# Order of work where stages meet in a four-layer attention and mixture kernel: norm transposes into the banks of keys and units, dense products around the last probabilities, the last norm tile one step later

## The chip, the cores and the metric

The kernel runs on one core of a Trainium2 chip. The core has five engines that each take their instructions in order and meet only at semaphores: TensorE (PE, matrix products; PEld is its weight load), VectorE (DVE), ScalarE (ACT), GpSimd (POOL) and SyncE (SP, which issues the DMAs). The metric is the device time of one execution in microseconds.

## The reference

`x` is 16 x 64 tokens of width 512, `ctx` as many. Four layers follow each other, each an attention and a mixture, each with a residual add and a layer norm ahead of it:

```python
x = x + _L0_xattn_ref(_layernorm(x), ctx, Wq, Wk, Wv, Wo)    # 32 heads, 4 key heads, keys = ctx and x
x = x + _L0_ffn_ref(_layernorm(x), base_W, gate_W, A, B)      # xf @ base_W.T + low-rank experts, top 2 of 28
x = x + _L1_xattn_ref(_layernorm(x), ctx, mask, ...)          # 32 heads, 8 key heads, rms-normed q and k
x = x + _L1_ffn_ref(_layernorm(x), W_base, gate_W, A, B)      # the same with top 2 of 8
x = x + _L2_xattn_ref(_layernorm(x), ctx, ctx)
x = x + _L2_ffn_ref(_layernorm(x), router_w, A, B)
x = x + _L3_xattn_ref(_layernorm(x), ctx, ...)
x = x + _L3_ffn_ref(_layernorm(x), weight, bias, centroids, assignments)

def _L0_ffn_ref(x, base_W, gate_W, lora_A, lora_B):
    base = xf @ base_W.T
    top_vals, top_idx = jax.lax.top_k(xf @ gate_W.T, TOP_K)
    top_probs = jax.nn.softmax(top_vals / TEMP, axis=-1)
    gate_full = zeros.at[arange, top_idx].add(top_probs)
    h = einsum('nd,erd->ner', xf, lora_A) * (gate_full * SCALING)[:, :, None]
    return base + einsum('ner,eor->no', h, lora_B)
```

## The kernel before

The 1024 tokens are eight tiles of 128 rows (`NT` = 8); `x` stays in SBUF. Every product is made in single precision out of three passes over a high and a low half of each operand (`PASSES`): ScalarE copies the high half (`..._hi`), VectorE or GpSimd subtracts it for the low half (`..._lo`, `low`).

**Attention.** `attention(a, next_ln)` runs 64 steps (`STEPS`; 8 head groups by 8 tiles) and one more, then a tail. Step t works on four tiles at once: projections of step t, `scores` of t-1, `p_transpose` and `attend` of t-2, `out_proj` of t-3. In the first layer the queries are made in units (`q_unit`) into the banks psQ and psT, half of the heads for two tiles each. psTP is two banks, psT and psP.

**Norms.** A tile's norm is `ln_stats` (VectorE), `ln_rstd` (GpSimd), `ln_norm` into `xn` (VectorE), `ln_transpose` (TensorE, four transposes into the bank that `ln_bank` names), `ln_hi` (ScalarE) and `ln_lo` (VectorE). The next layer's norm begins inside the attention: tiles 0 to 4 at steps 60 to 64 (`LN_SLOT`), tiles 5 and 6 in the tail, tile 7 in the loop after it.

**Mixture.** `ffn_step(f, next_ln, t)` runs for t = 0 to 10: `gate_product(f, t)` into psQ, `gates` (some ten small instructions of VectorE with one `gate_exp` of ScalarE between) that give `hid`, `hidden_transpose`, `hidden_hi`, `hidden_lo`, then `experts` onto the same bank as `dense_product(f, t)`. `ring3` names that bank, one of three. `experts_add` adds it to `x`.

**What sets the order.** Nothing but the order of the code in each engine's block; a wait on a semaphore holds all that stands behind it on that engine. At the end of an attention TensorE has `scores`, `p_transpose`, `out_proj` and `attend` of the last steps, and as work that depends on none of them the first gate and dense products and the norm transposes.

**The start.** SyncE loads `x` tiles 0 and 1, four slices of the first query weights, the context, the first key weights and then the other six tiles. GpSimd makes the low halves of two slices of the query weights (`low_wq`), of half the context (`low_ctx`) and of the key weights (`low_wkv`), VectorE the others. `idle_products(n)` are n products whose result nobody reads.

Names with a number in the rows below: L775 `q_unit`, L790 `q_proj`, L812 `kv_proj`, L822 `q_transpose`, L840 `p_transpose`, L850 and L856 `attend`, L869 `out_proj`, L706 `ln_transpose`, L720 `gate_product`, L733 `dense_product`, L955 `hidden_transpose`, L971 `experts`, L1721 every low half on VectorE, L488 every low half on GpSimd.

## Time and profile before

| what | us |
|---|---|
| median of 3 runs (1569.87 to 1570.59) | 1570.47 |
| the profiled execution, its own time | 1570.53 |
| its span, first to last instruction | 1568.7 |
| TensorE busy | 1501.3 |
| VectorE busy | 1008.9 |
| ScalarE busy | 821.1 |
| GpSimd busy | 379.4 |

The profiled execution spends 1.83 us outside its span. The first attention runs to about 641 us, its mixture to 686, the second attention to 1301, its mixture to 1346. A row of a timeline gives the start, the length, engine, line, operation, the tiles out<-in, shape and count, and in brackets how long the engine stood idle before it and who released it. Matrix products overlap, so the distance of two starts tells what one costs in a row of work.

### The profile page before, as it was taken

To read this page: it belongs to the slowest core of one execution; us is meant where nothing else is said; L and a number is where in the kernel's file an instruction comes from. 1 tells how busy PE (TensorE), PEld (TensorE's weight loads), DVE (VectorE), ACT (ScalarE), POOL (GpSimd) and SP (SyncE) were. 2 spreads that over 40 slices of the span, in tenths; PEclk is the share of its full clock that TensorE was granted. 3 is DMA by queue.
4 is the path that set the end of the run, shared out by engine and by line. 5 is a ranking of instruction groups with operands and counts; after the bars stand their busy time and mean duration, and the time that the engine had idled before them with its cause. 6 is when DMAs were issued, how large, how long until landed. Compare 5 with 4: busy or idle time off the path is not lost.

```text
span 1568.7 us, 27791 instructions
## 1 busy us (share of the span) xinstructions
PE 1501.3 (96%) x9658; PEld 1323.4 (84%) x9658; DVE 1008.9 (64%) x2475; ACT 821.1 (52%) x2862; POOL 379.4 (24%) x388
## 2 busy tenths in 40 slices
PE   7999999999999998999999999999999998879896
PEld 7899999999999997788888888888888887667785
DVE  6666556655665568766665666656666677688775
ACT  4556445644555455346565556555565652554542
POOL 4102010201111011133232332323232321543420
PEclk9999999999999999999999999999999998799998
DMA  4100100100011001010101010101100001111001
GB/s 182 62 28 28 42 28 28 56 14 28 28 55 36 33 13 41 28 41 28 41 28 41 28 50 19 68 8 62 41 28 32 5 8 55 44 55 35 24 11 57
DMA packets 14624, 60.21 MB, mean 38 GB/s; under 512 B 2085, under 2 KB 3493, under 8 KB 9497
## 3 DMA queue, kind: packets, MB, share of 16 engines
q1 hardware_dynamic: 14488, 58.46, 10.5%
q8 instruction: 79, 1.29, 0.4%
q14 instruction: 57, 0.46, 0.1%
HBM read 56.36 MB, written 2.10 MB: 37 GB/s over the span
## 4 chain that ended last, share of the span: by engine, by line
PE 59%; issue 27%; DVE 7%; POOL 3%; ACT 2%; DMA 1%; POOLq 0%; DVEq 0%; SPq 0%; ACTq 0%
PE psY L869 15%; PE psQ L790 11%; PE psKV L812 8%; PE psSO L759 3%; PE psSO L856 2%; PE psTP L822 2%; PE psQ L775 2%; PE psTP L775 2%; PE psSO L760 2%; POOL wo L488 1%; PE psTP L840 1%; PE psKV L733 1%; PE psQ L1137 1%; PE psQ L720 1%; PE psTP L706 1%
## 5 line engine op out<-in xcount | busy, mean ns | idle before, releaser
L869 PE MATMUL psY<-wo,oT 128*128 128x512 f32 x1536 | 384.9, 399 | 1.8 <-DVE oT L1721 1.2
L869 PEld LDWEIGHTS psY<-wo,oT 128*128 128x128 f32 x1536 | 278.6, 188 | 65.8 <-POOL wo L488 2.2
L488 POOL TENSOR_TENSOR wo<-stage_o,wo 128x512 fp32r<-128x512 f32 (+2 forms) x71 | 91.1, 1309 | 309.0 <-ACT wo L1275 309.0
L1275 ACT ACTIVATE pT<-psTP 128x512 fp32r<-128x512 f32 (+1 forms) x128 | 62.8, 491 | 169.4 <-PE psTP L840 169.4
L593 POOL TENSOR_TENSOR rms<-ms_eps,minus_half 128x5 f32<-128x5 f32 x64 | 74.7, 1168 | 280.2 <-DVE ms_eps L1884 277.2
L1356 ACT ACTIVATE prob<-wide,neg_mx 128x128 f32<-128x128 f32 x256 | 99.8, 391 | 75.0 <-DVE neg_mx L1871 74.8
L1353 ACT ACTIVATE prob<-s_sb,neg_mx 128x64 f32<-128x64 f32 x256 | 86.0, 337 | 98.3 <-DVE neg_mx L1871 98.3
L1721 DVE TENSOR_TENSOR pT<-psTP,pT 128x512 fp32r<-128x512 f32 (+1 forms) x128 | 71.3, 557 | 77.4 <-ACT pT L1275 76.4
L1721 DVE TENSOR_TENSOR v<-psKV,v 128x128 fp32r<-128x128 f32 x64 | 18.7, 292 | 140.4 <-ACT v L1275 140.4
L812 PEld LDWEIGHTS psKV<-wkv,arena 128*128 128x128 f32 x768 | 99.8, 190 | 9.0 <-DVE kT L1908 4.6
L812 PE MATMUL psKV<-wkv,arena 128*128 128x256 f32 x768 | 103.4, 284 | 1.2 <-DVE kT L1908 1.2
L790 PE MATMUL psQ<-wq,hT 128*128 128x512 f32 x384 | 104.0, 408 | 0.0
L775 PE MATMUL psQ<-hT,wq 128*128 128x256 f32 x768 | 99.6, 285 | 4.2 <-DVE hT L1721 2.9
L790 PE MATMUL psQ<-hT 128*128 128x512 f32 x372 | 100.1, 407 | 0.0
L775 PEld LDWEIGHTS psQ<-hT,wq 128*128 128x128 f32 x768 | 94.9, 192 | 5.9 <-DVE hT L1721 3.1
L812 PE MATMUL psKV<-wkv,hT 128*128 128x256 f32 x768 | 99.8, 286 | 0.0
L775 PE MATMUL psTP<-hT,wq 128*128 128x256 f32 x768 | 99.1, 286 | 0.0
L1275 ACT ACTIVATE oT<-psSO 128x512 fp32r<-128x512 f32 (+1 forms) x132 | 76.4, 579 | 38.8 <-PE psY L869 32.1
L775 PEld LDWEIGHTS psTP<-hT,wq 128*128 128x128 f32 x768 | 96.0, 195 | 0.0
L812 PEld LDWEIGHTS psKV<-wkv,hT 128*128 128x128 f32 x768 | 94.1, 192 | 0.3
L1326 ACT ACTIVATE pT<-psQ 128x128 fp32r<-128x128 f32 x252 | 66.3, 280 | 53.4 <-PE psQ L790 53.4
L1721 DVE TENSOR_TENSOR oT<-psSO,oT 128x512 fp32r<-128x512 f32 (+1 forms) x132 | 88.7, 672 | 7.5 <-ACT oT L1275 7.2
(303 smaller groups left out, 3389.5 us busy)
## 6 DMA issues: line engine op xcount, KB each, us to landing
stage_o<-in_wo SPq DMA_DIRECT2D x16, 1024.0 KB, 4.8
stage_q<-in_wq SPq DMA_DIRECT2D x15, 1024.0 KB, 5.3
stage_kv<-in_wkv SPq DMA_DIRECT2D x12, 512.0 KB, 3.6
stage_q<-in_ctx SPq DMA_DIRECT2D x16, 256.0 KB, 2.8
stage_o<-in_ctxT SPq DMA_DIRECT2D x2, 1024.0 KB, 5.8
stage_q<-in_base SPq DMA_DIRECT2D x2, 1024.0 KB, 4.9
...
```

Source lines behind the costliest of these rows:

```text
L488: g.tensor_tensor(dst[LO], stage, dst[HI].bitcast(f32), ALU.subtract).then_inc(ld[done or what + "_lo"], 1)
L593: g.tensor_tensor(rms[:, t.res(2)], ms_eps[:, t.res(2)], minus_half[:, 0:5], ALU.pow).then_inc(s["rms"], 1)
L759: mm(bank[:, at:at + 2 * keys], q_of(HI), k_of(slice(0, 2)), start=True, stop=False)
L775: m = mm(out, wq[:, wl, c, head], lat_pair(xl, c, k.res(NT) // 2), start=c == 0 and i == 0, stop=c == KT - 1 and i == 2)
L790: m = mm(by_eight(q_bank(st)[:]), lat(xl, k, n), wq_slice(st.div(NT) + a.wq0, wl, k), start=k == 0 and i == 0, stop=k == KT - 1 and i == 2)
L812: m = mm(psKV[:, b * 256:(b + 1) * 256], lhsT, wkv_k(wl, k, 256), start=k == 0 and i == 0, stop=k == KT - 1 and i == 2)
L869: m = mm(psY[:], oT[:, ol, h, :], wo[:, wl, h, :], start=h == 0 and i == 0, stop=h == HQ - 1 and i == 2)
L1275: copy = lambda o, i: nc.scalar.activation(o, i, ACT.Copy)
L1326: i = nc.scalar.activation(junk_q[h], q_bank(st)[:, h * HD:(h + 1) * HD], ACT.Square, accum_out=ssq[:, n, h:h + 1])
L1353: e = nc.scalar.activation(prob[:, at], s_sb[:, at], ACT.Exp, bias=neg_mx[:, j:j + 1], scale=1.0, accum_out=sums[:, j:j + 1])
L1356: e = nc.scalar.activation(prob[:, at], wide[:, at], ACT.Exp, bias=neg_mx[:, j:j + 1], scale=a.scale, accum_out=sums[:, j:j + 1])
L1721: return V.tensor_tensor(dst_lo, src, dst_hi.bitcast(f32), ALU.subtract)
```

## The change

It rewrites the order on all five engines at three places, with a few buffers moved so that the order is possible. What is computed stays the same, but for nine more idle products at the start.

- **Start.** `x` tiles 2 and 3 come in a DMA of their own ahead of the context, which then waits for the third weight slice. GpSimd takes a third slice of `low_wq` from VectorE and computes tiles 2 and 3's `ln_rstd` ahead of `low_ctx`; VectorE normalises tiles 2 and 3 ahead of its own `low_ctx`. 14 idle products in place of 5.
- **End of the first attention and its mixture.** The norm transposes of tiles 0 to 2 go to psKV, behind `out_proj` in place of ahead of it. `gate_product(0)` moves one step ahead; `dense_product(0)` stands behind the p_transpose of step 64 and `dense_product(1)` behind the last one; `hidden_transpose(0)` and `gate_product(1)` are in the tail, `dense_product(2)` one step later behind the transpose of tile 7. The halves of the experts' matrix are kept in `kT1` and `v1` in place of `wo`, and are made earlier (`high_b`, `low_b`). The base weights' halves (`next_wq`, `low_wq(8)`) are made behind the norm's in step 62.
- **Second attention.** The last `experts` of the first mixture stands inside the first `q_proj`; the transpose of norm tile 7 stands behind the second `q_proj`. At its end `gate_product(0)` moves ahead of `out_proj(61)`, `dense_product(0)` ahead of `attend(62)`, `dense_product(1)` ahead of the last `p_transpose`, and the mixture's head is as above; its experts' matrix is in the context part of `hT`.

The diff, cut to the lines that set the order:

```diff
-        if ln in (1, 3, 7):
-            return psT if n == NT - 1 and ln != 7 else psP
+        if ln == 1:
+            return psKV if n < 3 else psT
+        if ln in (3, 7):
+            return psT if n >= 4 and ln != 7 else psP
+        if ln == 2 and n == NT - 1:
+            return psP
...
-        return (psS, psKV, psY)[n % 3]
+        return (psKV, psS, psY)[n % 3]
...
+        sp.dma_start(x[:, 2:4], io["x"][:, 2:4]).then_inc(ld["x23"], 16)
+        sp.wait_ge(ld["slot2"], 16)
...
-        sp.dma_start(x[:, 2:NT], io["x"][:, 2:NT]).then_inc(ld["x_rest"], 16)
+        sp.dma_start(x[:, 4:NT], io["x"][:, 4:NT]).then_inc(ld["x_rest"], 16)
...
+        low("wq", halves(wq, 2), stage_q[:, 2], 3, "wq_lo_v")
+        ln_rstd(0, 2)
+        ln_rstd(0, 3)
...
-        for n in range(2, NT):
+        for n in range(4, NT):
...
-            if n == 3:
+            if n == 2:
                 low_wq(8)
+            if n == 5:
+                low_b(FF[0], 32)
...
+            if t.t == STEPS - 2:
+                low_b(FF[1], 66)
...
+            if f.index == 0 and t == 0:
+                pe.wait_ge(LNS[1]["lo"], ln_at(1, 3))
...
-                    pe.wait_ge(FS["x_add"], NT)
+                    pe.wait_ge(FS["x_add"], NT - 1)
...
-                        if not t.exists:
-                            gate_product(f, 0)
+                    if t1.exists and t.exists and not units:
+                        gate_product(f, 0)
...
+                    if not t.exists:
+                        dense_product(f, 0)
...
-                if a.norm_slot(t) == "between":
+                if a.rms and a.norm_slot(t) == "between":
...
+                if a.rms and not t.exists:
+                    gate_product(f, 0)
...
+                if not a.rms and a.norm_slot(t) == "between":
+                    ln_transpose(next_ln, t.t - LN_SLOT, lambda: ln_bank_free(next_ln, t.t - LN_SLOT, t2))
...
+                    dense_product(f, 0)
...
-                    ln_transpose(2, NT - 1, lambda: pe.wait_ge(LNS[2]["lo"], ln_at(2, NT - 1)))
+                    q_proj(t.back(-1), 0, 4)
+                    ln_transpose(2, NT - 1, lambda: None)
                 if t.exists and a.rms:
-                    if t.t < 2:
+                    if t.t == 1:
...
+            if not a.rms:
+                p_transpose(last)
+            pe.wait_ge(s["max"], last.c + 1)
+            dense_product(f, 1)
             if a.rms:
-                gate_product(f, 0)
-            pe.wait_ge(s["max"], last.c + 1)
-            dense_product(f, 0)
-            p_transpose(last)
+                p_transpose(last)
...
+            hidden_transpose(f, 0)
             ln_transpose(next_ln, 5, lambda: ln_bank_free(next_ln, 5, last))
-            dense_product(f, 1)
+            gate_product(f, 1)
...
-                if t == 1:
-                    pe.wait_ge(A["x_add"], (f.index + 1) * STEPS)
-                    dense_product(f, 2)
-                    ln_transpose(f.ln, NT - 1, lambda: None)
-                if t > 2:
+                    if t == 2:
+                        ln_transpose(f.ln, NT - 1, lambda: pe.wait_ge(LNS[f.ln]["lo"], ln_at(f.ln, NT - 1)))
+                        pe.wait_ge(A["x_add"], (f.index + 1) * STEPS)
                     dense_product(f, t)
-            if 0 <= u < NT:
+            if 0 <= u < NT - (f.index == 0):
...
-        idle_products(5)
+        idle_products(14)
...
-                if t.exists and not a.rms and not early and t.res(8) == 6:
+                if t.exists and not a.rms and not early and t.res(8) == 6 and t.t < LN_SLOT:
...
-                if a.norm_slot(t) == "between":
+                if a.rms and a.norm_slot(t) == "between":
                     ln_hi(next_ln, t.t - LN_SLOT)
+                if a.rms and t.t == STEPS:
+                    gate_exp(FF[1], 0)
+                if a.rms and t.t == STEPS:
+                    oT_hi(t2)
...
-                if t2.exists and a.rms:
+                if not a.rms and t.t == STEPS - 1:
+                    gate_exp(FF[0], 0)
+                if not a.rms and a.norm_slot(t) == "between":
+                    ln_hi(next_ln, t.t - LN_SLOT)
+                if t2.exists and t.exists and a.rms:
...
+                if not a.rms and t.t == STEPS - 2:
+                    next_wq(t)
...
+                if a.rms and t.t == STEPS - 3:
+                    high_b(FF[1], 17)
+                if not a.rms and t.t == STEPS:
+                    high_b(FF[0], 8)
...
-            gate_exp(FF[a.index], 0)
             oT_hi(last)
-            for n in range(5, NT - 1):
-                ln_hi(next_ln, n)
+            hidden_hi(FF[a.index], 0)
+            ln_hi(next_ln, 5)
+            gate_exp(FF[a.index], 1)
+            ln_hi(next_ln, 6)
...
-                for n in first:
+                for n in first if t.t > 0 else ():
...
+                    pT_lo(t2)
...
-                if t2.exists:
+                if t2.exists and not scores_first:
                     pT_lo(t2)
+                if a.rms and t.t == STEPS:
+                    gates(FF[1], 0)
...
-                if a.norm_slot(t) == "between":
+                if a.rms and a.norm_slot(t) == "between":
...
-                if t.exists and not a.rms and t.res(8) == 6:
+                if t.exists and not a.rms and t.res(8) == 6 and t.t < LN_SLOT:
                     low_wq(t.div(8) + 1)
+                ahead = a.rms and not t.exists
+                if ahead:
+                    x_add(t3)
+                    oT_lo(t2)
...
-                if t3.exists:
+                if not a.rms and t.t == STEPS - 1:
+                    gates(FF[0], 0)
+                if t3.exists and not ahead:
                     x_add(t3)
-                if t2.exists and a.rms:
+                if not a.rms and a.norm_slot(t) == "between":
+                    ln_lo(next_ln, t.t - LN_SLOT)
+                if t2.exists and a.rms and not ahead:
...
+                if not a.rms and t.t == STEPS - 2:
+                    low_wq(8)
...
-            gates(FF[a.index], 0)
...
+            hidden_lo(FF[a.index], 0)
...
+            gates(FF[a.index], 1)
...
-        def hidden_lo(f, n):
-            dve.wait_ge(FS["hidT_hi"], f.done + n + 1)
-            sub_hi(hidT[0:f.rows, LO, 0:f.parts], hid_bank(f, n)[0:f.rows].rearrange("p (j t) -> p j t", t=P),
-                   hidT[0:f.rows, HI, 0:f.parts]).then_inc(FS["hidT_lo"], 1)
...
-        low_wq(0, 2)
...
-        low_ctx(0)
...
+        ln_norm(0, 2)
+        ln_norm(0, 3)
+        low_ctx(0)
```

The changed file has other line numbers: L1770 there is L1721 here, L729 is L706, L743 L720, L758 L733, L870 L840, L899 L869, L997 L955 and L1013 L971.

**Start, VectorE.** Before, from the first normalised tiles to the queries of the first unit (x_res is `x`, stage_q the loaded query weights, stage_o the loaded context):

```order
L1721 TENSOR_TENSOR wq<-stage_q,wq 128x512
L1721 TENSOR_TENSOR hT<-psY,hT 128x4x128
L1721 TENSOR_TENSOR wq<-stage_q,wq 128x512
L1721 TENSOR_TENSOR hT<-psTP,hT 128x4x128
L1721 TENSOR_TENSOR hT<-stage_o,hT 128x4x2x64 x2
L1743 BN_STATS bn<-x_res 128x6
L1744 BN_AGGR mv<-bn 128x2
L1745 TENSOR_SCALAR var_eps<-mv 128x1
L1743 BN_STATS bn<-x_res 128x6
L1744 BN_AGGR mv<-bn 128x2
L1745 TENSOR_SCALAR var_eps<-mv 128x1
L1762 TENSOR_SCALAR xn<-x_res,mv,rstd 128x512 x2
```

and now:

```order
L1770 TENSOR_TENSOR hT<-psY,hT 128x4x128
L1770 TENSOR_TENSOR wq<-stage_q,wq 128x512
L1770 TENSOR_TENSOR hT<-psTP,hT 128x4x128
L1792 BN_STATS bn<-x_res 128x6
L1793 BN_AGGR mv<-bn 128x2
L1794 TENSOR_SCALAR var_eps<-mv 128x1
L1792 BN_STATS bn<-x_res 128x6
L1793 BN_AGGR mv<-bn 128x2
L1794 TENSOR_SCALAR var_eps<-mv 128x1
L1811 TENSOR_SCALAR xn<-x_res,mv,rstd 128x512 x2
L1770 TENSOR_TENSOR hT<-stage_o,hT 128x4x2x64 x2
```

One weight slice has left VectorE's list, and the statistics and the normalising of tiles 2 and 3 stand ahead of the two context slices.

**End of the first attention, TensorE.** Before, from the gate product of tile 0 (psQ<-wkv,hT) through the dense products 0 and 1 (psSO and psKV<-wq,hT):

```order
L720 MATMUL psQ<-wkv,hT 128x252 x12
L840 MATMUL psTP<-ident,prob 128x128 x4
L869 MATMUL psY<-wo,oT 128x512 x12
L850 MATMUL psSO<-pT,arena 128x256 x6
L706 MATMUL psTP<-ident,xn 128x128 x4
L733 MATMUL psSO<-wq,hT 128x512 x12
L840 MATMUL psTP<-ident,prob 128x128 x4
L869 MATMUL psY<-wo,oT 128x512 x12
L850 MATMUL psSO<-pT,arena 128x256 x6
L706 MATMUL psTP<-ident,xn 128x128 x4
L733 MATMUL psKV<-wq,hT 128x512 x12
L869 MATMUL psY<-wo,oT 128x512 x12
```

and now, from the same p_transpose as the second row above; the gate product of tile 0 stands one step further ahead:

```order
L870 MATMUL psTP<-ident,prob 128x128 x4
L758 MATMUL psKV<-wq,hT 128x512 x12
L899 MATMUL psY<-wo,oT 128x512 x12
L880 MATMUL psSO<-pT,arena 128x256 x6
L729 MATMUL psTP<-ident,xn 128x128 x4
L870 MATMUL psTP<-ident,prob 128x128 x4
L758 MATMUL psSO<-wq,hT 128x512 x12
L899 MATMUL psY<-wo,oT 128x512 x12
L880 MATMUL psSO<-pT,arena 128x256 x6
L997 MATMUL psTP<-ident,s_sb 112x128 x2
L729 MATMUL psTP<-ident,xn 128x128 x4
L743 MATMUL psQ<-wkv,hT 128x252 x12
```

Dense product 0 has moved between a p_transpose and the `out_proj` behind it, dense product 1 stands behind the last p_transpose, and a hidden transpose (s_sb) and the gate product of tile 1 stand ahead of the last `out_proj`.

**Head of the second mixture, TensorE.** Before, from the norm transpose of tile 6 to the dense product of tile 3 (psSO<-hT):

```order
L706 MATMUL psTP<-ident,xn 128x128 x4
L720 MATMUL psQ<-wkv,hT 128x72 x12
L955 MATMUL psTP<-ident,s_sb 64x128
L733 MATMUL psY<-hT 128x512 x12
L706 MATMUL psTP<-ident,xn 128x128 x4
L971 MATMUL psSO<-wo,oT 128x512 x3
L955 MATMUL psTP<-ident,s_sb 64x128
L720 MATMUL psQ<-wkv,hT 128x72 x12
L971 MATMUL psKV<-wo,oT 128x512 x3
L955 MATMUL psTP<-ident,s_sb 64x128
L720 MATMUL psQ<-wkv,hT 128x72 x12
L733 MATMUL psSO<-hT 128x512 x12
```

and now, from the same place:

```order
L729 MATMUL psTP<-ident,xn 128x128 x4
L1013 MATMUL psKV<-hT,qT 128x512 x3
L997 MATMUL psTP<-ident,s_sb 64x128
L743 MATMUL psQ<-wkv,hT 128x72 x12
L729 MATMUL psTP<-ident,xn 128x128 x4
L758 MATMUL psY<-hT 128x512 x12
L1013 MATMUL psSO<-hT,oT 128x512 x3
L997 MATMUL psTP<-ident,s_sb 64x128
L743 MATMUL psQ<-wkv,hT 128x72 x12
L758 MATMUL psKV<-hT 128x512 x12
```

Gate product 1 is in the tail, experts 0 (psKV<-hT,qT) comes first, and the transpose of tile 7 and dense product 2 (psY<-hT) now stand between gate product 2 and experts 1, where there was no dense product.

## Rows read from the trace of the kernel before

**Rows 1.** The page, part 1: busy time of each engine.

```profile
PE 1501.3 (96%) x9658; PEld 1323.4 (84%) x9658; DVE 1008.9 (64%) x2475; ACT 821.1 (52%) x2862; POOL 379.4 (24%) x388
```

**Rows 2.** Windows: stretch, length, busy of PE, PEld, DVE, ACT, POOL, PEclk, DMA.

```profile
52.00:583.70 531.70, 529.88 (x3809) 496.51 (x3808) 313.25 (x584) 276.14 (x832) 62.67 (x48) 1.00 0.09 31
583.70:694.86 111.16, 101.91 (x614) 88.25 (x613) 86.96 (x233) 51.01 (x128) 26.24 (x29) 1.00 0.12 42
1279.80:1322.31 42.51, 36.82 (x186) 29.26 (x185) 30.00 (x105) 9.25 (x31) 5.43 (x10) 0.88 0.15 50
1310.80:1322.31 11.51, 8.91 (x28) 6.92 (x29) 6.59 (x34) 0.98 (x5) 1.63 (x4) 0.56 0.15 49
1349.00:1366.00 17.00, 13.14 (x62) 12.33 (x61) 7.29 (x19) 7.53 (x17) 8.84 (x12) 0.51 0.11 32
```

**Rows 3.** Timeline of TensorE at the start.

```profile
11.99 3.14 PE L775 MATMUL psQ<-hT,wq 128*128 128x256 f32 x24 [2.87 <-DVE hT L1721]
18.96 1.12 PE L706 MATMUL psTP<-ident,xn 128*128 128x128 f32 x4 [3.82 <-DVE xn L1762]
...
20.58 4.71 PE L775 MATMUL psTP<-hT,wq 128*128 128x256 f32 x24
25.13 3.04 PE L812 MATMUL psKV<-wkv,hT 128*128 128x256 f32 x24
```

**Rows 4.** Timeline of VectorE at the start.

```profile
8.73 1.41 DVE L1721 TENSOR_TENSOR wq<-stage_q,wq 128x512 fp32r<-128x512 f32 x1 [1.50 <-ACT wq L1275]
...
10.66 0.68 DVE L1721 TENSOR_TENSOR wq<-stage_q,wq 128x512 fp32r<-128x512 f32 x1
...
16.26 0.69 DVE L1743 BATCH_NORM_STATS2 bn<-x_res 128x6 f32<-128x512 f32 x1 [0.80 <-DMA x_res<-in_x]
...
18.35 1.23 DVE L1762 TENSOR_SCALAR xn<-x_res,mv,rstd 128x512 f32<-128x512 f32 x2
```

**Rows 5.** Timeline of GpSimd at the start.

```profile
6.83 2.75 POOL L488 TENSOR_TENSOR wq<-stage_q,wq 128x512 fp32r<-128x512 f32 x2 [0.18 <-ACT wq L1275]
...
14.87 2.93 POOL L488 TENSOR_TENSOR wkv<-stage_kv,wkv 128x512 fp32r<-128x512 f32 x2
```

**Rows 6.** Who TensorE waited for in 583 to 611: total, times, longest.

```profile
PE psTP L706 <- DVE pT L1721: 2.3, 3, 1.0
```

**Rows 7.** Timeline of TensorE at the end of the first attention.

```profile
621.13 1.61 PE L720 MATMUL psQ<-wkv,hT 128*128 128x252 f32 x12
...
626.50 0.60 PE L706 MATMUL psTP<-ident,xn 128*128 128x128 f32 x4
626.85 3.00 PE L733 MATMUL psSO<-wq,hT 128*128 128x512 f32 x12
629.69 0.60 PE L840 MATMUL psTP<-ident,prob 128*128 128x128 f32 x4
```

**Rows 8.** Timeline of TensorE, three places of the first join.

```profile
619.00 0.98 PE L850 MATMUL psSO<-pT,arena 128*128 128x256 f32 x6 [1.97 <-DVE pT L1721]
...
652.31 0.43 PE L955 MATMUL psTP<-ident,s_sb 128*112 128x128 f32 x2 [1.34 <-DVE s_sb L1778]
...
694.86 0.60 PE L822 MATMUL psTP<-ident,q_sb 128*128 128x128 f32 x4
```

**Rows 9.** Timeline of VectorE, a norm and a query tile of this join.

```profile
616.78 1.57 DVE L1762 TENSOR_SCALAR xn<-x_res,mv,rstd 128x512 f32<-128x512 f32 x1
...
693.53 0.68 DVE L1892 TENSOR_TENSOR q_sb<-psQ,rms 128x512 f32<-128x512 f32 x1
```

**Rows 10.** Timeline of TensorE in the second mixture.

```profile
1313.40 0.42 PE L955 MATMUL psTP<-ident,s_sb 128*64 128x128 f32 x1 [2.61 <-DVE s_sb L1778]
1313.50 2.75 PE L720 MATMUL psQ<-wkv,hT 128*128 128x72 f32 x12
1316.06 5.42 PE L733 MATMUL psSO<-hT 128*128 128x512 f32 x12
...
1322.31 0.30 PE L955 MATMUL psTP<-ident,s_sb 128*64 128x128 f32 x1
```

89 lines of the change are left out of this document (50 added, 39 removed).

## The prediction, made before the change was run

> **What bounds the kernel now.** I read the page first: TensorE is busy 1501.3 us [rows 1] of a span of 1568.7, the others far less. So only two things can move the time: TensorE's idle and the clock it runs at, since the change takes no product away. Next the windows [rows 2]: from 52 to 583.7 us TensorE is busy 529.88 of 531.70 at full clock, and nothing is to be had. The stretch where the first attention hands over to its mixture and to the second attention (583.70 to 694.86) has 111.16 - 101.91 = 9.25 us of idle, the end of the second attention with the head of its mixture (1279.80 to 1322.31) 42.51 - 36.82 = 5.69 us and a granted clock of 0.88. Then the timelines, for who is late in each.
>
> **The start.** The idle of 3.82 us ahead of the transposes of norm tiles 2 and 3 [rows 3] ends with VectorE's xn at 18.35, whose statistics begin at 16.26, when the DMA has landed [rows 4]; the clock has fallen meanwhile: the unit behind it takes 4.71 us, the one ahead 3.14 [rows 3]. I walk the new order. GpSimd does two weight slices from 6.83 in 2.75 us, so 1.37 each; a third ends at 6.83 + 4.1 = 10.95 [rows 5]. VectorE's one remaining slice is ready at about 9.85 and reads stage_q and wq as GpSimd does. The trace has such a slice at 1.41 us beside GpSimd and 0.68 alone [rows 4]; 8.73 + 1.41 is 0.56 past GpSimd's end at 9.58, so I take it as held until GpSimd ends: 10.95 + 0.68 = 11.6. The low half of norm tile 1 ends 0.6 later, and the first unit starts at 12.25 in place of 11.99: the slice taken off VectorE gains nothing here. The unit ends at 15.3. Statistics of tiles 2 and 3 take 18.35 - 16.26 = 2.1 us [rows 4], from 12.2 to 14.3 (512 KB of x ahead of the context have landed by then: the 1536 KB behind it landed at 16.26); rstd and xn add 0.6 each, so the transposes run from 15.4 to 16.1, and the second unit follows at once, without the clock's fall, to 19.0. The first key product needs GpSimd's context and key slices. They end now about 14.9 + 2 x 2.93 = 20.8 (a pair of slices 2.93 [rows 5], the context's like the keys'; they wait for rstd of tile 3). So it starts at 20.85 in place of 25.13 [rows 3]: **4.3 us** gained. New idle there is 20.85 - 19.0 = 1.8 us; nine more idle products run in an idle that exists. Ends: if the slices do not collide, the first unit starts at 11.2 and all is 1.1 earlier (5.4); if the clock falls in the 1.8 us, about as before, 4.71 - 3.14 = 1.6 is given back (2.7). The Trainium skill (SBUF — State Buffer, section "Who interferes with whom") says that a VectorE instruction with two SBUF inputs fully blocks against a GpSimd one that reads SBUF. By that rule the slice ends at 11.6 as above; if the row's 1.41 were a mere slowing it would end at 9.85 + 1.41 = 11.3 and the start would gain 0.3 more.
>
> **End of the first attention.** (a) Norm transposes of tiles 0 to 2 waited for the low half of pT, which frees psP: 2.3 us in three waits [rows 6]. In psKV behind `out_proj` they wait for neither it nor xn (ready before out_proj's 2.84 us are over), so all of that goes and TensorE is 2.0 us early at the scores of step 62; it loses 0.3 there to the low half of the last unit. (b) VectorE is next late. Of the wait of 1.97 us ahead of attend [rows 8] one part was xn at 1.57 us in place of 0.55, held by GpSimd's weight slices [rows 9]. That collision goes, but VectorE's own two slices, 0.68 each [rows 4], now run at that time, and the first waits about 0.4 for GpSimd's; so pT's low half comes at 617.4, TensorE has arrived at 615.5, and it waits 1.9 us again. `out_proj(60)` ahead of it waits 0.85. (c) Behind that stand gate product 0 (622.57 - 621.13 = 1.44) and dense product 0 (629.69 - 626.85 = 2.84) [rows 7] as cover: dense 0 hides the ten small instructions of the gates, which now stand ahead of x_add and the low half of oT (2.1 us). `attend(62)` waits 0.7 and the last p_transpose 0.85. (d) In the tail hidden transpose 0, gate product 1 and experts 0 are covered; the transpose of tile 7 waits about 1.3 for the last statistics, rstd and xn; the wait of 1.34 for hid at 652.31 [rows 8] goes. By this walk TensorE is at that hidden transpose at 649.0: 3.3 us ahead. `high_b`, `low_b` (2.7 us of GpSimd) run while VectorE and TensorE need nothing of either; the rstd behind them on GpSimd is asked for 3 us later. If that cover is gone, it costs up to 2.7 us.
>
> **Head of the second attention.** The last experts inside q_proj takes away its wait for the low half (0.5). The transpose of tile 7 behind the second q_proj takes away its wait for xn (0.45). But VectorE has that tile's low half ahead of q_sb of step 0 in its list: the chain transpose, high half (0.6), low half (0.7), q_sb (0.68 [rows 9]) now starts only when the q_proj is over, and q_transpose waits 2.0 us, where it followed at once at 694.86 [rows 8]. It starts at about 692.45, so this join gives **2.4 us**. Count: 9.25 us of idle become 0.25 + 0.85 + 1.9 + 0.7 + 0.85 + 1.3 + 2.0 = 7.85, four stops fewer at 0.15 each: 2.0, near the walk's 2.4. Bounds: 4.4 if the low half of tile 7 is out of q_sb's way, -1 if VectorE is a microsecond later at three of its stops than I have it.
>
> **Second attention's end.** Gate product 0 (1.4) ahead of `out_proj(61)` covers the wait for oT; dense 0 covers attend's pT; x_add and oT's low half are ahead of the last normalise, and dense 1 covers that. By the walk I find none of these waits left up to hid of tile 1 (0.4). The tile-7 transpose waits for the last statistics: 1.45. Then dense 2 (2.84) stands between gate product 2 and hid of tile 2, where 2.61 us were waited [rows 10]: the gates of tile 2 end at 1309.2 and TensorE arrives at 1309.2. Idle 5.69 to 1.85 is 3.85, and 0.3 for three stops fewer. With the wait goes what followed it: from 1310.80 the clock was at 0.56 [rows 2], the dense product took 5.42 against 3.00 at full [rows 7, 10], the gate product 2.75, about half of it lost: 2.4 + 1.3 = 3.7 us. Together **7.8 us**: TensorE at hidden transpose 3 at 1314.5 in place of 1322.31 [rows 10]. Bounds: 4.1 if the clock falls all the same in the waits that are left, 8.5 if the 1.45 are shorter. Behind it nothing is changed; the half clock of 1349 to 1366 [rows 2] stays in the sum as it was.
>
> **Sum.** 4.3 + 2.4 + 7.8 = 14.5 us. The profiled execution took 1570.53, within 0.1 of the median 1570.47: **1556.0 us**.
>
> **Rivals.** (1) The clock takes part back. New idle of 1.8 us at the start, and 1.3, 1.45 and 0.4 at the heads, may bring half clock for a while as 2.61 us did: 1.6 to 3.7 us, so 1557.6 to 1559.7. For it: idles of this size are left; against: the 1.97 us at 617 [rows 8] and all else of the 9.25 us of the first join ran at full clock [rows 2]. The Trainium skill (TensorE: Matmul & The Clock Gate, section "A second HAM failure mode: psum-queue depth-cycling") tells of a clock that swings when the engine idles shortly but often between groups of products; by that rule this rival would hold at all three places. (2) VectorE bounds both ends: it is busy 86.96 of the 111.16 us and 30.00 of the 42.51 [rows 2], in chains, so cover in TensorE's order only moves the stop. Then the first join gives nothing and the second 1.5 less: 1560. For it: rows 8 and 9; against: a fifth to a third of its time in both stretches is still idle. (3) The half clock of 1349 to 1366 does not come back, since it hangs on when the idle falls: 13.14 us busy at 0.51 would save some 4 net of waits: 1552. (4) **Slower than before.** Each us of product at half clock costs one more. If the stops of the first join (0.85, 1.9, 0.7, 0.85 within 15 us) let the clock fall at 612 and it stays down into the mixture, whose dense and gate products run to 686, each 1 us of full-speed work there costs 1 more; more than 14.5 + 3.1 = 17.6 us of them, so half clock until about 650, makes 1573.6 or more. Against it: the fall at 1310.8 mended itself after some 10 us of unbroken work. (5) It does not do what it says, the covers sit where nothing waits: within 0.2% of before.
>
> **How the numbers follow.** Forecast 0.57; (1) 0.17; (2) 0.13; (3) 0.07; (4) 0.03; (5) 0.03. The forecast's own spread from the bounds (the start 2.7 to 5.4, join 1 -1 to 4.4, join 2 4.1 to 8.5) is about 2.5 us each way. The range reaches from (3), 1551.5, to (2) with a microsecond over, 1561.0. A measurement can tell about 0.2%, 3.1 us, from no change: faster 0.93, same 0.04, slower 0.03.
>
> **What would show it.** Right: the first L812 product near 20.9 with a second unit of 3.1 us; no wait of the norm transposes at steps 60 to 62; attend of step 61 still waiting near 2 us for pT; q_transpose of the second attention waiting 2 us for q_sb; hidden transpose 3 of the second mixture at full clock, 14 us earlier than before. Wrong: a granted clock below 0.9 in the windows around 18 to 25 or 1290 to 1310, or stops for oT or hid in the tails that I have at none.

## The result

| | before | after |
|---|---|---|
| median of 12 runs | 1571.06 | 1563.16 |
| lowest to highest | 1569.75 to 1574.84 | 1557.71 to 1568.28 |
| the profiled execution, its span | 1568.7 | 1560.7 |
| mean granted clock in it | 0.985 | 0.984 |

The ratio is 0.995, 95% interval 0.994 to 0.996: 7.9 us faster, where 14.5 was forecast, and 2.2 us outside the range. Half clock below means the lower of the two levels at which TensorE's clock is granted, 1.2 in place of 2.4 GHz, a PEclk of 0.5 in the windows. Two things stand out before any row. The kernel after spreads over 10.6 us, more than the 7.9 us that it gained. And its mean granted clock is no better than that of the kernel before, though 5.3 of the 14.5 us were to come from the clock (3.7 in the second mixture, 1.6 at the start).

The page of after, parts 1 and 2 (TensorE is as busy as in [rows 1], but for some idle products and for products that ran at half clock):

```profile
PE 1505.0 (96%) x9676; PEld 1326.3 (85%) x9676; DVE 1006.9 (65%) x2474; ACT 819.2 (52%) x2862; POOL 381.2 (24%) x389
...
PEclk9999999999999999999999999999999999799998
```

How far after is ahead of before at the same product of the program, from both timelines of TensorE:

| the product | before | after | ahead by | forecast |
|---|---|---|---|---|
| first key product | 25.13 | 21.06 | 4.07 | 4.3 |
| hidden transpose 2, first mixture | 652.31 | 644.87 | 7.44 | 7.6 |
| q_transpose of step 0, second attention | 694.86 | 687.83 | 7.03 | 6.7 |
| q_transpose of step 3 | 717.85 | 713.24 | 4.61 | 6.7 |
| q_transpose of step 63 | 1279.25 | 1274.75 | 4.50 | 6.7 |
| hidden transpose 3, second mixture | 1322.31 | 1311.44 | 10.87 | 14.5 |
| first attend of the cross-attention | 1465.93 | 1454.92 | 11.01 | 14.5 |
| end of the span | 1568.7 | 1560.7 | 8.0 | 14.5 |

Up to 687.83 us the walk holds to a third of a microsecond. From there 6.8 us are lost, 6.5 against the forecast since after was 0.3 ahead of it. They go in three steps: 2.5 behind the second attention's head, nearly all within 25 us, 1.4 in the second join (6.37 gained, not 7.8), 2.9 behind 1419 us, where the two kernels have the same instructions.

The windows of after, for the same stretches (columns as in [rows 2]; the last three are stretches cut out at half clock):

```profile
579.70:687.83 108.13, 101.47 (x617) 88.22 (x615) 84.61 (x233) 49.95 (x130) 26.49 (x29) 1.00 0.12 44
687.83:713.24 25.41, 22.44 (x128) 19.30 (x129) 13.79 (x40) 15.29 (x71) 8.53 (x7) 0.87 0.12 40
1275.30:1311.44 36.14, 34.25 (x186) 27.26 (x185) 28.95 (x105) 8.42 (x30) 4.18 (x9) 0.95 0.03 10
1419.00:1560.70 141.70, 124.77 (x649) 99.46 (x648) 95.38 (x251) 58.88 (x152) 40.51 (x56) 0.94 0.10 34
...
689.20:692.70 3.50, 3.26 (x16) 3.26 (x16) 0.88 (x2) 1.61 (x12) 0.00 (x0) 0.52 0.02 5
1300.20:1303.70 3.50, 3.06 (x10) 2.62 (x11) 3.29 (x16) 0.84 (x3) 0.81 (x2) 0.52 0.00 0
1453.80:1460.70 6.90, 5.78 (x14) 4.53 (x15) 2.79 (x7) 1.59 (x4) 0.81 (x2) 0.51 0.14 40
```

and of before, for the second and the fourth of these:

```profile
694.86:720.00 25.14, 21.87 (x142) 18.42 (x141) 15.65 (x43) 16.49 (x74) 9.83 (x8) 1.00 0.13 43
1430.00:1568.70 138.70, 120.69 (x649) 96.08 (x649) 95.34 (x251) 58.89 (x152) 40.49 (x56) 0.97 0.10 35
```

The head of the second attention had a clock of 1.00 in the kernel before and has 0.87 now; the second join 0.88 before [rows 2], now 0.95; what lies behind 1419 us (1430 before) had 0.97 and has 0.94. The second join parts waits from clock: TensorE's idle there went from 5.69 to 1.89 us (36.14 - 34.25), where 1.85 was forecast, but its busy time fell only from 36.82 to 34.25, 2.57 us, where 4.0 was forecast (3.7 of clock and 0.3 for stops fewer). In each of the three losses there is half clock. TensorE's timeline of after there:

```profile
685.23 0.60 PE L729 MATMUL psTP<-ident,xn 128*128 128x128 f32 x4
687.83 0.66 PE L850 MATMUL psTP<-ident,q_sb 128*128 128x128 f32 x4 [2.01 <-DVE q_sb L1946]
...
689.44 2.93 PE L840 MATMUL psKV<-wkv,arena 128*128 128x256 f32 x12 [0.84 <-DVE kT L1962]
...
702.31 0.67 PE L850 MATMUL psTP<-ident,q_sb 128*128 128x128 f32 x4 [1.71 <-DVE q_sb L1946]
702.80 0.39 PE L857 MATMUL psKV<-ident,k_sb 128*128 128x128 f32 x1
702.85 2.91 PE L818 MATMUL psQ<-hT 128*128 128x512 f32 x6
...
1300.64 1.11 PE L729 MATMUL psTP<-ident,xn 128*128 128x128 f32 x4 [1.33 <-DVE xn L1811]
1301.41 4.00 PE L758 MATMUL psY<-hT 128*128 128x512 f32 x12
...
1454.92 1.65 PE L1188 MATMUL psY<-kT,pT 128*128 128x512 f32 x3 [2.67 <-DVE pT L1770]
```

and of before, at the second, fourth and last of these:

```profile
696.41 1.69 PE L812 MATMUL psKV<-wkv,arena 128*128 128x256 f32 x12 [0.84 <-DVE kT L1908]
...
707.93 0.66 PE L822 MATMUL psTP<-ident,q_sb 128*128 128x128 f32 x4 [1.71 <-DVE q_sb L1892]
708.42 0.27 PE L829 MATMUL psKV<-ident,k_sb 128*128 128x128 f32 x1
708.45 1.63 PE L790 MATMUL psQ<-hT 128*128 128x512 f32 x6
...
1465.93 0.96 PE L1152 MATMUL psY<-kT,pT 128*128 128x512 f32 x3 [2.67 <-DVE pT L1721]
```

Read them in pairs. The same twelve key products take 1.69 and 2.93 us behind the same stop of 0.84; after has its new stop of 2.01 us 1.6 us ahead of them, which before has not. The same q_transpose, behind the same stop of 1.71, is followed by full clock before and by half clock after. The same attend behind the same stop of 2.67 took 0.96 and takes 1.65. The stops were read rightly; for the last two, what the clock does behind them is not the same each time.

### The profile page after: what moved, and what is told of

It is laid out like the page before. It is cut to its first block, busy times and chain, and to the rows that moved or that the text cites. A ratio compares the mean times of both kernels' runs of the same rounds, so it can differ in the third digit from the quotient of the medians.

```text
span 1560.7 us, 27827 instructions
## 1 busy us (share of the span) xinstructions
PE 1505.0 (96%) x9676; PEld 1326.3 (85%) x9676; DVE 1006.9 (65%) x2474; ACT 819.2 (52%) x2862; POOL 381.2 (24%) x389
## 4 chain that ended last, share of the span: by engine, by line
PE 60%; issue 26%; DVE 8%; POOL 3%; ACT 2%; DMA 0%; SPq 0%; POOLq 0%; DVEq 0%; ACTq 0%
PE psY L899 14%; PE psQ L818 11%; PE psKV L840 8%; PE psSO L787 3%; PE psSO L886 2%; PE psTP L850 2%; PE psSO L788 2%; PE psQ L803 1%; POOL wo L506 1%; PE psTP L870 1%; PE psTP L803 1%; PE psSO L758 1%; PE psQ L1173 1%; PE psKV L1217 1%; DVE hT L1770 1%
## 5 line engine op out<-in xcount | busy, mean ns | idle before, releaser
L899 PE MATMUL psY<-wo,oT 128*128 128x512 f32 x1536 | 384.7, 399 | 1.4 <-DVE oT L1770 0.8
L899 PEld LDWEIGHTS psY<-wo,oT 128*128 128x128 f32 x1536 | 278.3, 188 | 65.7 <-POOL wo L506 2.3
L506 POOL TENSOR_TENSOR wo<-stage_o,wo 128x512 fp32r<-128x512 f32 x68 | 87.3, 1313 | 309.2 <-ACT wo L1311 309.2
L1770 DVE TENSOR_TENSOR pT<-psTP,pT 128x512 fp32r<-128x512 f32 (+1 forms) x128 | 71.2, 556 | 75.9 <-ACT pT L1311 75.1
L1770 DVE TENSOR_TENSOR v<-psKV,v 128x128 fp32r<-128x128 f32 x64 | 18.6, 291 | 142.3 <-ACT v L1311 142.3
L840 PEld LDWEIGHTS psKV<-wkv,arena 128*128 128x128 f32 x768 | 101.0, 192 | 8.3 <-DVE kT L1962 3.7
L840 PE MATMUL psKV<-wkv,arena 128*128 128x256 f32 x768 | 104.5, 286 | 0.8 <-DVE kT L1962 0.8
L840 PE MATMUL psKV<-wkv,hT 128*128 128x256 f32 x768 | 99.9, 286 | 1.0 <-POOL wkv L506 1.0
L840 PEld LDWEIGHTS psKV<-wkv,hT 128*128 128x128 f32 x768 | 94.0, 192 | 1.5 <-POOL wkv L506 1.2
L506 POOL TENSOR_TENSOR wq<-stage_q,wq 128x512 fp32r<-128x512 f32 x35 | 44.9, 1294 | 204.5 <-ACT wq L1311 165.8
```

The costliest lines, as they stand in the source:

```text
L506: g.tensor_tensor(dst[LO], stage, dst[HI].bitcast(f32), ALU.subtract).then_inc(ld[done or what + "_lo"], 1)
L840: m = mm(psKV[:, b * 256:(b + 1) * 256], lhsT, wkv_k(wl, k, 256), start=k == 0 and i == 0, stop=k == KT - 1 and i == 2)
L899: m = mm(psY[:], oT[:, ol, h, :], wo[:, wl, h, :], start=h == 0 and i == 0, stop=h == HQ - 1 and i == 2)
L1770: return V.tensor_tensor(dst_lo, src, dst_hi.bitcast(f32), ALU.subtract)
```

## Experiments

Two theories. **Clock**: the walk over waits was right, and half clock behind TensorE's stops took back what it had given. **Waits**: something in the order that the walk missed (VectorE's chains, a stop that moved) costs the 6.5 us. Medians, spreads and mean granted clocks of the single runs:

| kernel | median | lowest to highest (n) | clocks | ratio to before, 95% |
|---|---|---|---|---|
| after | 1563.16 | 1557.71 to 1568.28 (12) | 0.980 to 0.989 | 0.995 [0.994, 0.996] |
| e1_start | 1569.52 | 1565.87 to 1571.93 (12) | 0.983 to 0.990 | 0.998 [0.997, 0.999] |
| e2_head_order | 1557.42 | 1553.64 to 1562.34 (6) | 0.983 to 0.993 | 0.992 [0.990, 0.993] |
| e3_head_fill | 1562.18 | 1557.37 to 1565.23 (6) | 0.983 to 0.993 | 0.994 [0.992, 0.996] |
| e5_all_fill | 1562.18 | 1561.43 to 1563.27 (6) | 0.994 to 0.997 | 0.994 [0.993, 0.996] |
| e6_dense_first | 1563.05 | 1558.38 to 1565.37 (6) | 0.982 to 0.991 | 0.994 [0.993, 0.996] |
| e7_short_fill | 1551.21 | 1550.47 to 1552.49 (4) | 0.995 to 0.998 | 0.987 [0.986, 0.989] |
| e8_before_fill | 1564.75 | 1563.78 to 1566.52 (5) | 0.990 to 0.994 | 0.996 [0.995, 0.997] |
| e9_head_and_fill | 1549.84 | 1548.09 to 1551.89 (4) | 0.995 to 0.998 | 0.987 [0.985, 0.988] |
| e10_fill_no_start | 1555.25 | 1554.73 to 1556.99 (4) | 0.994 to 0.996 | 0.989 [0.987, 0.990] |
| e11_before_more_fill | 1563.53 | 1561.23 to 1566.18 (6) | 0.992 to 0.997 | 0.994 [0.993, 0.996] |
| e12_best | 1549.33 | 1548.56 to 1550.35 (4) | 0.996 to 0.998 | 0.986 [0.984, 0.987] |

The ratios are to the kernel before, run beside each group: its median was 1571.27 beside e1 to e5, 1569.98 beside e6 to e9 and 1572.21 beside e10 to e12. So a microsecond or two between medians of two groups shows little, and the ratios are known to 0.1 to 0.2%, 1.6 to 3 us.

Within one kernel the time follows the clock: of after's twelve runs the fastest (1557.71) had 0.989 and the slowest (1568.28) 0.980.

### The start alone

The kernel before with the start's part of the diff.

> The kernel before with the change of the start alone. Theory (the walk was right, TensorE's clock took the rest): the first key product starts at 21.06 us as in the profile after, in place of 25.13, and everything up to 1310 us stands 4.05 us earlier; half clock behind 1300 us may fall elsewhere than before, so the span is 1564.7, give or take 3. Rival (the gains of the parts do not add up, the start's is lost in the first attention already): less than 3 us left at step 60 (1228.4 us is where out_proj of step 61 of the second attention started before; 1223.6 here by the theory).

Its profile has the first key product at 21.61 and stands 3.18 ahead at 643 us and 3.13 at q_transpose 63, so the gain lasts through both attentions, 0.9 below what was written (the start itself came out at 3.5). At the end of the span nothing of it is left (1568.8 against 1568.7, where 1564.7 give or take 3 was expected): 6.8 us of half clock had come at 1461.9, behind the stop of 2.67 that ran through in the profile of before, and 3.4 at 1547.2. That is this one execution. Over the runs the medians are 1.8 us apart and the ratio gives 3.0 (1.3 to 4.9), so the start's gain may be there whole. The rival, less than 3 us left in the second attention, is out by the 3.13, narrowly.

### The wait for q_sb

```diff
+                if t.exists and a.rms:
+                    qk_normalise(t)
                 if a.index == 1 and t.static and t.t == 0:
                     ln_lo(2, NT - 1)
-                if t.exists and a.rms:
-                    qk_normalise(t)
```

> The changed kernel with one line moved on VectorE: at step 0 of the second attention q_sb and k_sb ahead of the low half of norm tile 7. Theory: the wait of 2.01 us of the first q_transpose goes nearly whole (0.7 left at most, then kT waits 0.84 as before), and with it the half clock of 689 to 692 us, which cost 1.3: the second attention runs 2.5 to 3.3 us earlier than in the profile after (out_proj of step 61 at 1219.5 to 1220.3 in place of 1222.8). Rival (the next wait takes over, p_transpose of step 0 then waits for the low half): under 1 us gained.

TensorE's timeline at the place:

```profile
685.24 0.60 PE L729 MATMUL psTP<-ident,xn 128*128 128x128 f32 x4
685.74 0.66 PE L850 MATMUL psTP<-ident,q_sb 128*128 128x128 f32 x4
...
687.51 1.70 PE L840 MATMUL psKV<-wkv,arena 128*128 128x256 f32 x12 [1.00 <-DVE kT L1962]
```

The wait of 2.01 is gone whole, and both half clocks of this head with it: q_transpose 0 is 2.1 us earlier than in after, q_transpose 63 4.1 us (1270.64 against 1274.75), 0.8 beyond the expectation, since the half clock of 703 went too. The median is 5.7 us below after's. It is the one line of order that the change lacked at this place.

### The same wait, filled

Idle products (`ident` by `ident`, 128 columns, into a bank that is free) stand in the wait, which stays:

```diff
+        def fill(bank, count):
+            for _ in range(count):
+                mm(bank[:, 0:P], ident[:], ident[:], start=True, stop=True)
...
+                if st.static and st.t == 0:
+                    pe.wait_ge(LNS[2]["lo"], ln_at(2, NT - 1))
+                    fill(psT, 14)
```

> The changed kernel with 14 idle products (128 columns, 0.117 us each at the start, so 1.6 us) in the wait of 2.01 us ahead of the first q_transpose of the second attention; the wait itself stays. Theory (half clock follows on stops, whatever TensorE computes in them): q_transpose starts at 687.8 as before, but the 12 key products behind it take 1.7 in place of 2.93 us and the half clock of 689 to 692 is gone: 1.2 us gained there; that of 703 has its own stop of 1.71 and may stay. Rival (the clock falls for another reason than the stop): products at 689.4 still take 2.9.

```profile
686.04 3.29 PE L722 MATMUL psTP<-ident 128*128 128x128 f32 x28
...
690.72 1.69 PE L844 MATMUL psKV<-wkv,arena 128*128 128x256 f32 x12 [0.84 <-DVE kT L1967]
...
702.24 0.66 PE L855 MATMUL psTP<-ident,q_sb 128*128 128x128 f32 x4 [1.71 <-DVE q_sb L1951]
```

The fourteen took 3.29 us, 0.235 each (two instructions each), not 0.117: q_transpose came at 689.17, some 1.0 us later than the wait would have let it. Yet the key products behind are over at the same time as in after (690.72 + 1.69 = 692.41 against 689.44 + 2.93 = 692.37), because they ran at full clock. The expected 1.2 us of clock is there, spent on fill that was too long. One profile each way would be little, for the clock differs between executions; but all of them agree here. The two that have the stop of 2.01 as it is, after and e6_dense_first, have half clock behind it, e6 for 10.2 us from 688.0:

```profile
690.02 2.93 PE L840 MATMUL psKV<-wkv,arena 128*128 128x256 f32 x12 [0.84 <-DVE kT L1963]
```

The seven in which it is filled or gone (e2, e3, e5, e7, e9, e10, e12) have none there. So the half clock hangs on the stop. The half clock of 703 is absent in e3 behind its own unchanged stop of 1.71. e5_all_fill has the same program up to 1298 us and got it. A window of e5_all_fill, and the same of e3_head_fill:

```profile
701.90:705.30 3.40, 3.35 (x11) 2.86 (x12) 1.46 (x4) 3.40 (x12) 1.39 (x2) 0.50 0.00 0
```

```profile
701.90:705.30 3.40, 3.06 (x17) 2.62 (x18) 1.75 (x5) 3.40 (x13) 1.10 (x1) 1.00 0.00 0
```

The same program up to there and the same stop ahead, the clock 0.50 in one execution and 1.00 in the other.

### All long stops filled, too long and then right

> The changed kernel with idle products in all its longer stops from 686 us on: 14 ahead of the first q_transpose of the second attention, 10 ahead of the tile-7 transpose of the second mixture, in the middle 10, 16 and 13 at 1335.5, 1340.1 and 1346, 28 at 1395.5, 11 at 1392, in the cross-attention 20, 13 and 11 at 1452, 1526 and 1537. All waits stay as they are. Theory (clock): of the 45 us or so at half clock of the profile after (17 of them from 1338 on) most come back at full clock; each us of busy time at half clock was worth half a us, less what is then waited: 8 to 15 us faster than the changed kernel, 1548 to 1555 us, and a spread of single runs well below the 10 us of the changed kernel. Rival (the stops are not what lets the clock fall, or the idle products delay what waits): no gain, 1561 or more.

> The changed kernel with idle products as in e5_all_fill, but half as many: one idle product took 0.21 us at full clock there (it is two instructions), not 0.117, so those of e5_all_fill ran past the waits that they stood in. Now 8 ahead of the first q_transpose of the second attention, 5 ahead of the tile-7 transpose, 5, 8 and 7 in the middle, 15 and 6 around 1395, 11, 7 and 6 in the cross-attention, each by its count x 0.21 within the wait. Theory (clock): half clock stays away as there (21.5 us in that profile against 51.0 in the changed kernel's), and nothing is delayed: 1550 to 1556 us, spread of single runs under 5 us. Rival (what the idle products of e5_all_fill gave back in clock was not worth anything, since the stretches from 1338 on are bound by VectorE): 1560 or more.

Where e5 had 28 idle products in the stop of 3.66 us and 20 in that of 2.67, e7 has 15 and 11; the edit in the cross-attention stands for the others:

```diff
+                need(pe, s["x_add"], n)
+                fill(psY, {0: 11, 6: 7, 7: 6}.get(n, 0))
                 pe.wait_ge(s["pT_lo"], n + 1)
                 pe.wait_ge(s["f_lo"], n + 1)
-                need(pe, s["x_add"], n)
```

e5 kept most of the clock (0.994 to 0.997) and the spread fell from 10.6 to 1.8 us, but the median was only 1 us below after's: the fill held up what it stood ahead of. TensorE's timeline of e5 at the first stop of the middle (ten products, in half clock that came all the same, 4.03 us in a wait of 1.41), then of e7 at the tile-7 transpose, at that first stop and at the first attend:

```profile
1336.68 4.03 PE L722 MATMUL psTP<-ident 128*128 128x128 f32 x20
1340.46 1.68 PE L1130 MATMUL psSO<-arena,kT 128*128 128x256 f32 x12
```

```profile
1298.06 1.36 PE L722 MATMUL psSO<-ident 128*128 128x128 f32 x10
1299.56 0.66 PE L733 MATMUL psTP<-ident,xn 128*128 128x128 f32 x4
...
1332.92 1.28 PE L722 MATMUL psTP<-ident 128*128 128x128 f32 x10
1334.50 1.70 PE L1129 MATMUL psSO<-arena,kT 128*128 128x256 f32 x12 [0.29 <-DVE kT L1787]
...
1446.66 2.62 PE L722 MATMUL psY<-ident 128*128 128x128 f32 x22
1449.50 0.97 PE L1205 MATMUL psY<-kT,pT 128*128 128x512 f32 x3 [0.22 <-DVE pT L1787]
```

With the length right e7 is 12.0 us faster than after (12.3 by the ratios), 1551.21, with no wait shortened. The second join now gives what was forecast: from q_transpose 63 (1273.66) to hidden transpose 3 (1309.01) 35.35 us against 43.06 before, 7.7 gained, forecast 7.8. Fill does not always hold the clock there: e5, and e9_head_and_fill with the same five idle products as e7, had half clock from 1299.2 and 1296.1, and e9 gains 6.4 in this stretch. The rival (the stretches from 1338 on are bound by VectorE anyway) is out.

### The kernel before, filled

> The kernel before with the idle products of e7_short_fill in the middle and the cross-attention, none earlier. Theory (clock, and it has nothing to do with the change): half clock of 17.1, 3.4 and 3.4 us from 1348 on goes: 5 to 9 us faster than the kernel before, 1562 to 1566. Rival: within 1 us of before.

1564.75, 5.2 us below the kernel before measured beside it (1569.98), as expected and nothing to do with the change. Against e7_short_fill, run beside it, it gives the change's worth with the clock held in most places: 1564.75 - 1551.21 = **13.5 us**, where the forecast was 14.5. e7 is also filled at the head and in the second join, and this kernel is not; e11 below fills the stops that the change removes.

### The start undone, with the clock held

> e7_short_fill with the start of the kernel before (all other parts of the change kept). With the clock held in the stops from 686 us on, each part should show at its own size. Theory: 3.7 to 4.1 us slower than e7_short_fill, 1554.9 to 1555.3 us. Rival (what the start gives is taken back later by waits, as the start alone seemed to give only 1.8 us in e1_start): under 2 us slower, 1553 or less.

1555.25, 4.0 us above e7 (by the ratios to before 0.9889 and 0.9872, 2.7 us, since the kernel before came out 2.2 us apart beside the two). In the profiles the first key product is 3.7 us and hidden transpose 3 3.8 us later than in e7. The rows say that the start's gain lasts. That it is kept better with the clock held than in e1_start is not shown: the ratios give 3.0 us there and 2.7 here.

### How much of the change was clock

Idle products in the two stops of before that the change removes.

> e8_before_fill (the kernel before, idle products in middle and cross-attention) with idle products also where the change removed a stop: 15 in the stop of 3.8 us ahead of norm transposes 2 and 3, 10 in that of 2.6 us ahead of hidden transpose 2 of the second mixture. All waits stay; only the clock can be better. Theory (of the change's 13.5 us between e8_before_fill and e7_short_fill a good third is clock, the rest waits): the unit behind the first stop takes 3.1 in place of 4.7 us and the gate and dense products behind the second 4.4 in place of 8: 4 to 5 us faster than e8_before_fill, 1560 to 1561. Rival (it was all waits): 1564 to 1565.

```profile
15.42 3.51 PE L699 MATMUL psKV<-ident 128*128 128x128 f32 x30
...
20.68 3.12 PE L779 MATMUL psTP<-hT,wq 128*128 128x256 f32 x24
...
1311.87 4.13 PE L699 MATMUL psSO<-ident 128*128 128x128 f32 x20
...
1315.86 1.51 PE L724 MATMUL psQ<-wkv,hT 128*128 128x72 f32 x12
1317.20 3.03 PE L737 MATMUL psSO<-hT 128*128 128x512 f32 x12
```

Both places behave as expected: the unit takes 3.12 in place of 4.71 [rows 3] (3.81 in e8's profile), gate and dense product 1.51 and 3.03 in place of 2.75 and 5.42 [rows 10]. At hidden transpose 3 it is 3.0 us ahead of e8_before_fill. But the medians differ by 1.2 only (1563.53 and 1564.75), not by 4 to 5, and by the ratios (0.9942 and 0.9960, the kernels before beside the two being 2.2 us apart) by 2.8: the second fill met half clock itself (4.13 us for 20 instructions) and ran 1.3 over its wait, and two stretches of 3.4 us at half clock came at 1339.5 and 1346.3, which e8 had not. So some 3 us of the 13.5 are clock, by the rows and by the ratios, less than the third that was expected; the uncertainty of the ratios is about as large, and the rival, no gain, is not excluded by them. Against e7 the ratios leave 11.0 us for the change once the two stops that it removes are filled in the kernel before.

### The stop of 1.33 covered

```diff
                     if t == 2:
-                        ln_transpose(f.ln, NT - 1, ...)
                         pe.wait_ge(A["x_add"], (f.index + 1) * STEPS)
                     dense_product(f, t)
+                    if t == 2:
+                        ln_transpose(f.ln, NT - 1, ...)
```

> The changed kernel with dense product 2 ahead of the transpose of norm tile 7 in both mixtures, so that it stands where TensorE waited 1.34 us for xn in the second mixture (0.60 in the first). Theory (VectorE's chain is what ends this stretch: gates of tile 2 follow x_add, statistics and xn of the last tile and end at 1304.7 us): the wait for xn goes, and about 1.3 us appear ahead of hidden transpose 2 instead, so no more than 0.3 us are gained there. Rival (TensorE's order cost it): 1.3 us gained in the second mixture, 0.6 in the first.

The wait for xn is gone, and no wait came in its place: hidden transpose 2 stands 7.27 us behind hidden transpose 1, where it was 8.52 in after. That looks like the rival, but the dense product fell into half clock, though TensorE had stopped for no more than 0.43 us in the 20 us before:

```profile
1302.07 4.58 PE L758 MATMUL psY<-hT 128*128 128x512 f32 x12
...
1307.91 0.30 PE L997 MATMUL psTP<-ident,s_sb 128*64 128x128 f32 x1
```

and VectorE had its hid ready only then:

```profile
1307.38 0.28 DVE L1833 SCALAR_TENSOR_TENSOR s_sb<-psQ,small,gate 128x64 f32<-128x64 f32 x1
```

The 1.6 us that half clock cost the dense product lay where TensorE would have waited for hid: at full clock it would be there at 1306.3 and wait until 1307.7 (an estimate from these rows). e7, which keeps the stop at full clock, has 7.19 for the same stretch. So VectorE's chain does end this stretch, and half clock cost next to nothing here. The median is after's. My expectation named the wait, and did not see that half clock can hide in it.

### Both put together

> The changed kernel with q_sb and k_sb ahead of the low half of norm tile 7 as in e2_head_order, and the idle products of e7_short_fill from 1290 us on. Theory: both gains add: 1557.4 of e2_head_order less what the clock gives from 1290 on, 5 to 8: 1550 to 1553 us. Rival: no better than e2_head_order, 1557.

> e9_head_and_fill with idle products in three more places: 7 in the stop of 1.71 us ahead of q_transpose of step 2 of the second attention (half clock came at 699 in e9), and more of them in the middle (6, 12, 11 for 5, 8, 7), where 0.3 to 1.3 us of stop were left. Theory: the half clock of 699 goes, 1 us; the middle was at full clock already: 1548 to 1549.5. Rival (each idle product put in costs as much as it brings): 1550 or more.

1549.84 and 1549.33, 14.9 us below after for e12 by the ratios. e12 has no half clock left up to 1540 us (0.998 in its profile, span 1546.8), and its median is in the expected range; that of e9 is 0.2 below its own. The two cannot be told apart. e12 is the fastest kernel of this study, 0.986 of before (0.984 to 0.987) and by the medians 13.8 us below the changed kernel.

## Why the prediction was wrong

**Start: right.** Forecast 4.3, measured 4.07 (3.7 by the rows of e10 and e7). Timelines of after, of TensorE, VectorE and GpSimd in turn:

```profile
15.10 0.60 PE L729 MATMUL psTP<-ident,xn 128*128 128x128 f32 x4
16.55 0.66 PE L729 MATMUL psY<-ident,xn 128*128 128x128 f32 x4 [0.85 <-DVE xn L1811]
16.96 3.11 PE L803 MATMUL psTP<-hT,wq 128*128 128x256 f32 x24
21.06 3.14 PE L840 MATMUL psKV<-wkv,hT 128*128 128x256 f32 x24 [0.99 <-POOL wkv L506]
```

```profile
9.91 1.54 DVE L1770 TENSOR_TENSOR wq<-stage_q,wq 128x512 fp32r<-128x512 f32 x1
...
15.00 1.49 DVE L1811 TENSOR_SCALAR xn<-x_res,mv,rstd 128x512 f32<-128x512 f32 x1 [0.45 <-POOL rstd L519]
```

```profile
14.94 2.70 POOL L506 TENSOR_TENSOR hT<-stage_o,hT 128x512 fp32r<-128x512 f32 x2
```

The second unit at 3.11 and full clock and GpSimd's key slices as the bound are as walked. The weight slice on VectorE ended at 11.45, between the 11.3 of a mere slowing and the 11.6 of the rule that the Trainium skill gives (SBUF — State Buffer, "Who interferes with whom"), and settles nothing. What the walk had not: xn of tile 3, priced at 0.6, took 1.49 beside GpSimd's first context slice, so the unit starts at 16.96 and not at 16.1. It cost nothing, since the key slices end later still. Nor did the nine more idle products, which the walk put into idle time, where half clock stretched them: in e5 and e7 the 14 took 4.87 and 4.76 us in place of 3.29 and the first unit began at 13.7, and the first key product still came at 21.03 and 21.39.

**First join: right.** The walk named seven stops; they came as 0.29, 0.79, 1.60, 0.76, 0.62, 0.60 and 2.01 us (forecast 0.25, 0.85, 1.9, 0.7, 0.85, 1.3, 2.0). The transposes of norm tiles 0 to 2 wait no more for pT, which was 2.3 us [rows 6]. TensorE was to be 2.4 us further ahead at q_transpose 0 than at the start, and is 2.96.

**The step that failed** is the one behind that stop. The prediction let the new wait of 2.0 us for q_sb cost 2.0 us and went on at full clock. It was followed by half clock at 689, 1.4 us, and the old stop of 1.71 by half clock at 703, 1.0 us, where before had full clock. That the stop of 2.01 is the cause of the first, e2 and e3 show: taken away or filled, the key products take 1.7 us again, and so in all seven profiles without it. The prediction had no term for either; its bounds for this join spoke of waits alone, and even rival (1), which lists the idles that might bring half clock (1.8, 1.3, 1.45 and 0.4), leaves out this one, the longest.

**Second join: the mechanism right, the size off by the clock.** The waits for oT, hid of tile 2 and the rest went as walked, and 0.44 and 1.33 stayed (forecast 0.4 and 1.45): idle 1.89 for 1.85. Mis-sized is the term of 3.7 us for the clock, which with 0.3 for stops came to 2.57, because half clock came again at 1300.2: 6.4 us gained in place of 7.8. (The 0.3 for three stops fewer is also not the 0.15 each of the first join.) In e7, with full clock here, it is 7.7. Whether the stop of 1.33 brought the half clock stays open: it came in the three profiles that have the stop as it is, but also in e5 and e9, where it is filled (in e5 but for 0.72 us), and in e6, where it is gone.

**Behind it** the prediction had "nothing is changed", and so no term. Nothing is changed in the instructions, but after lost 2.9 us to half clock at 1453.8 and 1539, stretches that had run at full clock in the profile of before. The half clock of 1349 to 1366 [rows 2] did come back, as forecast (17 us of it from 1337.7); e2 and e3 have 13.6 us of it in two pieces and e6 6.8, so that was a draw too.

**The error behind the three.** I took the granted clock for a property of the program and counted each half clock of one profile as a gain once its stop was gone. Across executions the same stop is followed by half clock or not, so a faster kernel gets a new draw at every stop that is left. Counted over the profiled executions of all 13 kernels, half clock that begins in a stop or at most 1.5 us behind it:

| stop of TensorE | left as it is | filled or gone |
|---|---|---|
| 2.0, first q_transpose of the second attention, order after | 2 of 2 | 0 of 7 |
| 2.6 to 2.8, hidden transpose 2 of the second mixture, order before | 3 of 3 | 1 of 1 |
| 1.3, transpose of norm tile 7 there, order after | 3 of 3 | 3 of 6 |
| 2.7, first attend of the cross-attention | 3 of 6 | 0 of 7 |
| 1.7, q_transpose of step 2 of the second attention | 8 of 12 | 0 of 1 |
| 2.0, attend of step 61 of the first attention, order before | 2 of 4 | |

The last row is the stop that the prediction took as evidence against rival (1), since it ran at full clock in the one profile that it had; in e8 and e11 half clock came 1.2 and 1.5 us behind it, at 619.7 and 619.3. Its argument against rival (4), that the fall at 1310.8 mended itself "after some 10 us of unbroken work", read the 10 us wrongly: the half clock ran from 1311.1 to 1321.3 and its first 2.3 us were the stop itself.

Rival (1) was this, with 0.17 and 1.6 to 3.7 us; it should have been the likeliest case, and with a price for every stop above 1.3 us in the program, those behind the change among them.

The section cited from the Trainium skill (TensorE: Matmul & The Clock Gate, "A second HAM failure mode: psum-queue depth-cycling") tells of a clock that swings between its two levels when TensorE idles shortly but often between groups of products. The trace agrees on the swings, nine stretches at half clock in after's profile; here most come at single stops of 1.3 to 3.7 us within work that is otherwise dense. Of the prediction's own signs of being wrong neither clock window showed it: 1.00 in 18 to 25 us and 0.91 in 1290 to 1310. The loss lay at places that it had not listed.

The waits alone, 14.5 - 5.3 = 9.2 us, lie within what the runs allow for two kernels of the same mean clock (7.9; by the interval of the ratio 6.3 to 9.4). That agreement is in part luck, for the mean clock of either kernel is itself a draw.
